# Attention and ternary FFN on eight cores: the first phase shifted by one stage, f and the normalized input transposed by DMA, the ternary weights made in the first phase

## The reference

```python
x = x + attn(layernorm(x))        # x: [8, 4096, 1024] float32
x = x + ffn(layernorm(x))

def attn(x):
    f = x @ W.T + b
    e = f @ f.T + clip(abs(i - j), 0, 10) * 0.01
    return softmax(e, axis=-1) @ f

def ffn(x):
    scale = max(mean(abs(weight)), 1e-5)
    w = clip(round(weight / scale), -1, 1)
    return x @ (w * scale).T
```

## Time and profile before

| what | value |
|---|---|
| median of 3 runs (range) | 1038.83 us (1037.99 to 1039.6) |
| the profiled execution, its own time | 1042.26 us |
| its span, slowest core | 1040.7 us |
| spans of the eight cores | 1024.7 to 1040.7 us |
| TensorE busy | 969.1 us, 93% |
| VectorE busy | 566.4 us, 54% |
| ScalarE busy | 369.7 us, 36% |
| GpSimd busy | 158.9 us, 15% |
| mean granted TensorE clock, slowest core | 0.970 |
| DMA | 186.88 MB, 180 GB/s |

### The profile page before, as it was taken

How to read it: one execution, slowest core, us unless ns; L and a number is a source line. 1 busy time by engine, 2 the same in 40 slices (tenths; PEclk the granted TensorE clock), 3 DMA queues, 4 the chain that set the end, 5 groups by cost and what they waited for, 6 DMA issues and landing times.

```text
span 1040.7 us, 15748 instructions; the slowest of 8 cores (1024.7 to 1040.7 us)
## 1 busy us (share of the span) xinstructions
PE 969.1 (93%) x4958; PEld 471.7 (45%) x4958; DVE 566.4 (54%) x923; ACT 369.7 (36%) x519; POOL 158.9 (15%) x160
## 2 busy tenths in 40 slices
PE   7799999999999979855999999999999999999996
PEld 6354554545445434322444444444444444444442
DVE  5456658685858358453344354545455554556532
ACT  3466656555445645401222323232222222232300
POOL 4000000000000000000001021221324243444530
PEclk9899999999999989978999999999999999999997
DMA  8524423444414656787889897989878888878320
GB/s 230 183 72 135 148 95 139 146 140 149 141 64 157 185 160 212 220 249 215 199 239 234 227 250 211 254 201 249 198 217 227 201 232 180 231 166 236 72 83 40
DMA packets 214897, 186.88 MB, mean 180 GB/s; under 512 B 106656, under 2 KB 181664, under 8 KB 212896
## 3 DMA queue, kind: packets, MB, share of 16 engines
q1 hardware_dynamic: 147584, 127.17, 44.7%
q10 hardware_dynamic: 67200, 58.72, 19.8%
q0 software_dynamic: 32, 0.00, 0.0%
HBM read 109.06 MB, written 51.38 MB: 154 GB/s over the span
## 4 chain that ended last, share of the span: by engine, by line
PE 62%; DVE 12%; SPq 9%; DMA 9%; ACT 4%; issue 3%; DVEq 0%; ACTq 0%
PE pb L652 30%; PE pb L406 12%; PE pb L709 11%; PE pb L359 7%; SPq L281 6%; DMA ln2T<-ln 5%; DVE rm L431 4%; DVE cmax L435 3%; DMA xb<-ft 2%; SPq L345 2%; ACT er L423 1%; PE pt L265 1%; DVE lnb L321 1%; DMA escr<-er 1%; DMA xe<-x 1%
## 5 line engine op out<-in xcount | busy, mean ns | idle before, releaser
L406 PE MATMUL pb<-fT 128*128 128x512 bf16 (+3 forms) x1152 | 242.2, 366 | 0.6 <-ACT fT L369 0.6
L652 PE MATMUL pb<-f,pTa 128*128 128x512 bf16 x1024 | 229.8, 382 | 13.8 <-DVE o L664 13.8
L652 PE MATMUL pb<-f,pTb 128*128 128x512 bf16 x1024 | 229.0, 381 | 0.0
L406 PEld LDWEIGHTS pb<-fT 128*128 128x128 bf16 x1152 | 109.8, 99 | 114.1 <-issue 6.3
L652 PEld LDWEIGHTS pb<-f,pTa 128*128 128x128 bf16 x1024 | 100.8, 100 | 128.4 <-issue 17.1
L652 PEld LDWEIGHTS pb<-f,pTb 128*128 128x128 bf16 x1024 | 100.7, 99 | 114.1 <-issue 2.4
L709 PE MATMUL pb<-wqT,ln2T 128*128 128x512 bf16 x512 | 120.4, 390 | 18.4 <-DVE wqT L777 11.0
L540 ACT ACTIVATE p<-eB,negm 128x3968 bf16<-128x3968 f32 (+30 forms) x31 | 62.1, 2002 | 199.3 <-DMA pTa<-p 99.2
L359 PE MATMUL pb<-ln1T,WT 128*128 128x512 bf16 x512 | 116.8, 388 | 9.3 <-ACT fT L369 7.9
L664 DVE SCALAR_TENSOR_TENSOR o<-pb,st,xres 128x512 f32<-128x512 f32 x64 | 48.0, 751 | 141.9 <-PE pb L652 141.5
L423 ACT COPY er<-pb 128x512 f32<-128x512 f32 (+2 forms) x128 | 69.9, 546 | 79.5 <-PE pb L406 40.9
(11 more groups left out here) (79 smaller groups left out, 631.6 us busy)
## 6 DMA issues: line engine op xcount, KB each, us to landing
escr<-er SPq DMA_DIRECT2D x105, 256.0 KB, 2.3
xres<-x SPq DMA_DIRECT2D x32, 512.0 KB, 5.4
out<-outb SPq DMA_DIRECT2D x32, 512.0 KB, 6.5
xb<-x SPq DMA_DIRECT2D x28, 512.0 KB, 4.3
xb<-ft SPq DMA_DIRECT2D x16, 512.0 KB, 5.6
wst<-wt SPq DMA_DIRECT2D x8, 512.0 KB, 8.8
escr<-eB SPq DMA_DIRECT2D x15, 256.0 KB, 3.2
eB<-escr ACTq DMA_DIRECT2D x2, 1792.0 KB, 11.0
```

Source lines behind the costliest of these rows:

```text
L406: inst = e.matmul(bk[:, 0:n], fT[:, h * S + I * P:h * S + (I + 1) * P], fT[:, h * S + c0:h * S + c0 + n], start=(h == 0), stop=(h == NH - 1))
L652: inst = e.matmul(bank[nb][:, :], pT[I % 2][:, j * P:(j + 1) * P], f_sb[:, j * D + nb * 512:j * D + (nb + 1) * 512], start=(pos == 0), sto ...
```

## The change

- Phase one: chunk 0 and chunk 1 are projected first, in halves of 256 rows (`fproj(c, h, u)`), with the score groups of chunk 0 between them (their evictions, `egroup_out`, emitted later through the list `late`). After that `stage(c)` for c from 1 to 7 emits the score groups of chunk c with the eight `fproj` of chunk c+1 spread evenly between them, and the layer norm of chunk c+2 in single steps at fixed slots.
- `ln1T` has two buffers. Tiles 8 to 31 of the input are transposed by DMA, tiles 0 to 7 still on TensorE. `ftrans(c, h)` is now a DMA transpose of 128 columns by 512 rows, eight per chunk, 64 in all. Row tile 0 of the second layer norm is still transposed on TensorE, in halves (`tail`).
- The stores of score groups with q above 0 are issued by ScalarE instead of SP.
- W is laid out on the host so that each of its eight loads reads whole rows of 4 KB; two of the eight casts go from GpSimd to ScalarE.
- The FFN weight is loaded once, into the buffers of W's float32 copy, in stage 1; `absum` in stage 2, `scale_prep` at its end, `quant` in stages 3 (four), 4 (two) and 5 (two), each slice stored to DRAM, and the whole loaded as bfloat16 (2 MB) into `wqT` after phase one by `wq_load`.
- What waited for the last TensorE instruction of phase one (`e_last_pe`) waits for it and for the DMA transposes of f (`fT_free`).
- Phase two: `ptrans(nn)` is emitted before the FFN of the row tile before and its store, not at the head of the next turn; for row 31 `mfin_col`, `mfin_tmp` and `sub` come at later marks; the tail works in halves of 512 columns with its own banks and stores, and statistics of row 0 come with its halves.

The core of the diff:

```diff
-                [fproj_pe.get(s // 4 - 1)])
+            if s >= 8:
+                xtr_tok[s] = ln1T_tok[s] = tdma(
+                    sl_xt[k], dst, lnb[k][:, :], apply_tok[s],
+                    fproj_pe[s // 4 - 2])
+                return
...
+        def ftrans(c, h):
+            dst = f_sb[:, 4 * c * D:4 * (c + 1) * D].rearrange(
+                "p (s x) -> p s x", s=4)[:, :, h * P:(h + 1) * P]
+            src = fT[:, h * S + c * 512:h * S + (c + 1) * 512]
...
+            t = tdma(sl_ft[c], dst, src, fT_tok[(c, NH - 1, 0)],
+                     fT_tok[(c, NH - 1, 1)], *free)
...
-            ts = SP.dma(slot, lambda e, w: e.dma_start(
+            ts = (ACT if q else SP).dma(slot, lambda e, w: e.dma_start(
...
-                wst[h].rearrange("p (c x) -> p c x", c=NH),
-                wt_d[:, h * P:(h + 1) * P].rearrange("(c p) x -> p c x", p=P)))
+                wst[h][:, :], wt_d[h]))
...
+        def stage(c):
+            es = [(I, q) for I in range(4 * c, 4 * c + 4)
+                  for q in range(nq(I))]
+            if c == NCH - 1:
+                es = [(I, q) for I in (31, 30, 29, 28) for q in range(nq(I))]
+            items = [lambda I=I, q=q: egroup(I, q) for I, q in es]
+            if c + 1 < NCH:
+                step = len(items) / NH
+                for h in range(NH - 1, -1, -1):
+                    items.insert(int(h * step + step / 2),
+                                 lambda h=h: fproj(c + 1, h))
+            n = len(items)
+            if c + 2 < NCH:
+                for k in range(4):
+                    for i, fn in enumerate(tile_tasks(4 * c + 8 + k)):
+                        at_slot(k * n // 4 + i, fn)
+            if c == 1:
+                for k in range(NH):
+                    at_slot(2 * k, lambda k=k: ft_load(k))
+            if c == 2:
+                for k in range(NH):
+                    at_slot(1 + 2 * k, lambda k=k: absum(k))
+                at_slot(n - 1, scale_prep)
+            for c_, i, k in ((3, 1, 0), (3, 4, 1), (3, 13, 2), (3, 19, 3),
+                             (4, 4, 4), (4, 18, 5), (5, 4, 6), (5, 20, 7)):
+                if c == c_:
+                    at_slot(i, lambda k=k: quant(k))
+            if c < NCH - 1:
+                for h in range(NH):
+                    at_slot(n * (h + 2) // 11 + 1, lambda h=h: ftrans(c, h))
...
+        fT_free += [e_last_pe[0]] + [f_tok[4 * c] for c in range(NCH)]
         res_load(31)
         loadE(29)
         rl(31)
         exp_col(30)
         exp_row(30)
         ptrans(30)
+        wq_load()
         loadE(28)
...
-                    ptrans(nx)
                     exp_col(nx)
...
+            if nn >= 0:
+                ptrans(nn)
             if not first:
                 ffn(pv)
-                final(pv)
+                if I:
+                    final(pv)
+        tail()
```

More of the change, by code:

```diff
@@ L422, in egroup, with egroup_out @@
                 free = er_free[r]
+            if late is not None:
+                late.append(lambda: egroup_out(
+                    I, q, i, r, n, c0, dst, slot, free, tp))
+            else:
+                egroup_out(I, q, i, r, n, c0, dst, slot, free, tp)
+        def egroup_out(I, q, i, r, n, c0, dst, slot, free, tp):
+            bk = bank[i]
             ta = ACT.op(lambda e, w: e.copy(dst, bk[:, 0:n]), tp, *free)
@@ L789, in build_nc, with ln_done @@
             x_load(s)
-        for h in range(NH):
+        for h in (1, 3, 4, 5, 6, 7):
             w_cast(h)
+        def ln_done(k, q=None):
+            ln_apply(k)
+            xtrans(k, q)
         ln_stats(0)
+        ln_rs(0)
         ln_stats(1)
-        ln_apply(0)
-        xtrans(0)
-        warm(8)
-        ln_apply(1)
+        ln_rs(1)
+        ln_done(0)
+        warm(9)
         ln_stats(2)
-        xtrans(1)
-        warm(8)
-        ln_apply(2)
+        ln_rs(2)
+        w_cast(0)
@@ L886, in build_nc @@
-        e_last_pe[0] = ftr_pe[NST - 1]
+        ln_rs(3)
+        fproj(0, 0, 0)
+        ln_done(2, DVE)
+        w_cast(2)
+        fproj(0, 1, 0)
+        fproj(0, 2, 0)
+        ln_done(3, DVE)
+        for u, h in ((0, 3), (1, 0), (1, 1), (0, 4), (1, 2), (0, 5), (1, 3),
+                     (0, 6), (1, 4), (1, 5), (0, 7), (1, 6), (1, 7)):
+            fproj(0, h, u)
+        emit_band()
+        late = []
+        ln_stats(4)
+        ln_rs(4)
+        ln_stats(5)
+        ln_rs(5)
+        egroup(0, 0, late)
@@ new lines, in build_nc @@
+        egroup(1, 0, late)
+        ln_done(4)
+        ln_stats(6)
+        ln_rs(6)
+        egroup(2, 0, late)
+        ln_done(5)
+        ln_stats(7)
+        ln_rs(7)
+        egroup(3, 0, late)
+        for fn in late[:2]:
+            fn()
+        fproj(1, 0, 0)
+        ln_done(6)
+        for fn in late[2:]:
+            fn()
+        fproj(1, 1, 0)
+        fproj(1, 2, 0)
+        ln_done(7)
+        for h in range(3, NH):
+            fproj(1, h, 0)
+            if h < 7:
+                fproj(1, h - 3, 1)
+            ftrans(0, h - 3)
@@ L887, in build_nc @@
+        for k in range(4):
+            for fn in tile_tasks(8 + k):
+                fn()
+        for c in range(1, NCH):
+            stage(c)
+        fT_free += [e_last_pe[0]] + [f_tok[4 * c] for c in range(NCH)]
         res_load(31)
@@ L899, in build_nc @@
                 if nx >= 0:
-                    ptrans(nx)
                     exp_col(nx)
                 ln2_moments(pv)
-            if nn >= 0:
+            if nn >= 0 and not first:
                 mfin_col(nn, last_cm)
```

339 lines of the change are left out of this document (178 added, 161 removed).

## The result

The changed kernel takes 1053.29 us (median of four runs, 1052.77 to 1056.91) against 1038.83 before: ratio 1.0147, interval 1.0123 to 1.0171. It is slower by 1.5%, clear of the noise; I had written 972 with 945 to 1002 and gave "slower" 3 in 100. The profiled execution has a span of 1051.6 us on core 3.

The account below looks back on a forecast made before the run. The prediction took TensorE, busy 93% of the span, as the bound. Savings of 32 (phase one), 23 (turn), 5 (later rows) and 6 (tail) took the span from 1040.7 to 975, written as 972 us, range 945 to 1002.

Parts of the forecast that it names:

- less behind it unless VectorE lags: Stages 1 to 7: waits for late tiles about 7 us after stage 1, 2 after stage 2, then less.
- the bounding engine: Phase one: 56 packs moved from TensorE to DMA take 25 us off TensorE, at 0.45 us each.
- Start: Beginning of phase one: stage 1 of the new order starts at 57.
- (a): Start: TensorE's own work before stage 1, 35.5 us from about 16, is done near 52.
- (b): Start: the last tile of chunk 2 is scaled at 50 and landed transposed at 57.
- Stages 1 to 7: Rest of phase one: 36, 37, 45.5, 47.5, 53.5, 59.6 and 53.5 us, 332.6 together.
- Clock: Stage 1: 2 us added for low clock, nothing in the stages behind it.
- The turn: Change to phase two: 75 us with stalls of 9 and clock 2, 23 us less than before.
- Rival 3: The turn does not shrink: p chain and DMA keep rows late, 10 of the 23 us remain, 985; chance 0.12.
- Later rows and tail: Phase two after the turn: 5 us less in the later rows and 6 us less in the tail.
- Rival 4: Stages 1 to 5: new transposes cost SP 5.2 us each like pTa's, 93 us more, 1065, slower; chance 0.03.
- Rival 2: Phase one: SP or DMA sets the pace, stages 1 to 5 lose 7 us more each, 35 in all, 1005; chance 0.15.

Follow-up runs that it names:

- e1: Changed kernel with the layer norm of tiles 8 to 11 emitted in steps between chunk 1's projections: ratio 0.9946 to the kernel before.
- e8: Changed kernel with tiles 8 to 11 interleaved, tiles in earlier slots with later scaling, ternary slices two a stage and ternary rows loaded earlier: ratio 0.9628 to the kernel before.
- e4: Changed kernel with input tiles 8 to 31 transposed on TensorE again (24 packs), f still by DMA: ratio 1.0706 to the kernel before.
- e10: Kernel before, with the 32 transposes of f by DMA instead of packs on TensorE, stage order unchanged: ratio 1.0060.
- e12: e8 with 28 packs of f (stages 0 to 6) back on TensorE: ratio 0.9669, core median 1003 against 1004 of the control.
- e9: Kernel before with two edits of phase two, p's transpose issued ahead of the out store and the tail in halves: ratio 0.9936.
- e11: Kernel before with the attention weights laid out so that each of the eight loads is whole 4 KB rows: ratio 0.9948.
- e6: Changed kernel with tiles 8 to 11 interleaved, tiles in earlier slots, and their root, scaling and transpose one slot later: ratio 0.9774 to the kernel before.
- edit 3: Ternary slices spread two a stage over stages 3 to 6; alone on the changed kernel, core median 1036, 10 us below it.
- the early loads: The eight loads of ternary rows moved before the scores of chunk 0, part of e8; not run apart.
- the later offsets: A tile's root, scaling and transpose one slot later (offsets 0, 2, 3, 4 in place of 0 to 3), part of e6; not run alone.

## Why the prediction was wrong

The step that failed first is how late a tile may be: "less behind it unless VectorE lags", with stalls of 7 and 2 us and then nearly none. Measured were waits of 21.0, 14.3, 6.2, 7.9 and 2.5 us for transposed tiles. The second is that 25 us of packs come off "the bounding engine" in full; the runs show none of them arriving. The third is the clock behind each stall, put at 2 us in all. By part:

**Start, predicted 57, measured 86.6.** Two terms failed. (a) "TensorE's own work up to there is done near 52": it was done at 65.7, with 40.4 us busy instead of 35.5 and 9.4 idle in waits that I had not counted. (b) "The last tile of chunk 2 landed transposed at 57": I reckoned VectorE's time alone. The tile's root needs ScalarE, and in ScalarE's list it stood behind chunk 1's evictions. The diff showed that; I never went through what is queued ahead of L319. The early tile (22 predicted) came at 26.7. Part (b) is worth 11 us of start (e1); the rest of the 30 is (a) and the tiles' own pace, not told apart.

**Stages 1 to 7, predicted 332.6 us together, measured 371.8.** Each stage was the larger of TensorE's and VectorE's load plus a stall. The loads were right (VectorE in stages 3 to 5: 35.9, 39.7 and 45.7 busy with 59, 63 and 73 gaps of 0.1, so 41.8, 46.0 and 53.0 against my 43.6, 47.4 and 53.5). What failed is "less behind it unless VectorE lags": an engine at 0.7 busy lags all the same, when its list asks for a tile's transpose 0 to 4 items before it is needed. In stages 4 and 5 this cost 9.7 and 11.4 us over the forecast. In stage 1, 7.5 over the forecast, it was SP: the last tile was scaled at 117.0 and its transpose issued at 124.1. With lists in better order (e8) the same seven stages take 413.9 - 76.2 = 337.7, 5 from the forecast. So the forecast was right for stages whose tiles have a lead, and this change gives them none.

**Clock, predicted 2 us for stage 1 and nothing behind it.** In the changed kernel one stall near 220 shows this: granted clock of windows of 2 us.

```profile
226.00:228.00 2.00, 2.00 (x6) 0.68 (x5) 0.00 (x0) 0.92 (x2) 0.00 (x0) 0.50 0.00 0
228.00:230.00 2.00, 2.00 (x9) 0.78 (x8) 0.00 (x0) 0.46 (x3) 0.00 (x0) 0.75 0.00 0
230.00:232.00 2.00, 2.00 (x11) 0.94 (x10) 1.24 (x2) 0.91 (x2) 0.00 (x0) 1.00 0.30 116
...
238.00:240.00 2.00, 2.00 (x9) 0.87 (x8) 1.59 (x5) 0.62 (x1) 0.00 (x0) 0.81 1.12 367
```

TensorE works again from 223.3 and gets 1.2 GHz until about 229: 3 us lost; then 2.4 GHz; then 0.81 to 0.86 for 5 us from 236: 1 more. So some 3 to 4 us for every such stall, and phase one had five (ending at 86.6, 130.2, 168.9, 223.3 and 282.0; the one at 168.9 is only 3.9 us long, at the scale's matmul), with a smaller one at 341.4. The whole can be read from e8, which has the same matmuls in phase one (compare the row of the changed kernel in run 4):

```profile
15.00:413.91 398.91, 356.77 (x1848) 177.23 (x1848) 281.58 (x466) 165.41 (x312) 6.81 (x6) 0.97 0.69 187
```

Of the 44.6 us between them 31.7 are idle time (73.9 to 42.1) and 12.8 busy time, which is the clock.

**Packs, "25 us less on the bounding engine".** This step carried the forecast's optimism. TensorE was busy 93% and so I let its time count in full. e10 shows none of 14.4 us arriving in the old order, e12 none of 12.6 in the new; both are packs of f, and for the 24 of the input e4 shows a price, but not in the packs' own time.

**The turn, predicted 75, measured 83.5 (before 98).** The weights' waits did go. TensorE's stalls are 19.2 us where I had 9. "What is late next" was named rightly, the chain of p, but mis-sized: the transpose of p(29) held SP 21.45 us where I had taken's chain plus 5. The same transpose held it 12.12 in the kernel before, in a row that I had not looked at (the earlier trace rows has only the other buffer of pT). I counted 2 MB less of loads, and not that scores, residual, weights and three transposes fall into 40 us of full DMA engines (0.99). Rival 3 (13 of the 23 us lost, 10 kept) had the direction: 8.5 were lost.

**Later rows and tail, predicted 11, measured 11.7.** Right, and e9 makes 7 to 9 of it alone.

**Transposes on SP.** Right: 1.24 to 1.32 us. Rival 4, the only one on the slower side, was priced by a cause that is not there; the Trainium skill's 1309 ns for a block ("VectorE: DVE Perf Modes", "The three transpose paths") is here about what an instruction with four or eight blocks holds SP, and eight blocks land 4.6 to 5.2 us after issue in the median, not eight times 1309 ns. The time came out on its side for another reason. Rival 2 had the size (35 us in stages 1 to 5; measured 32.4 over the forecast there) but laid all of it to SP and DMA. That is the mechanism in stage 1; in stages 4 and 5 SP issues the transpose 1.8 us after the scaling, and there the scaling itself is late.

The sum closes: 975 + 29.6 (start) + 39.2 (stages) + 8.5 (turn) - 0.7 (rest) = 1051.6, the profiled span.

**Where e8's gain over the kernel before lies**, core 5 of both (1029.6 and 1003.8): phase one 422.87 to 414.92, 8.0; from there to the end of the fifth FFN 129.3 to 122.5, 6.8; the rest 477.4 to 466.4, 11.0. The last piece is mostly e9's two edits. Of the first, e11's layout alone can bring 5, so the shift of the stages, the halves and 56 packs fewer are together worth about 3 on this core. Over all eight cores e8 starts phase two 7.7 to 15.1 us earlier, and with the spread of single cores named above those 3 are not told from nothing.

What stays open: whether e8 is faster than e6 at all, and by edit 3 or the early loads (not run apart); what the halves and the later offsets are worth; and what a turn with fewer bytes would give (not tried).

## What to carry to other kernels

Before shifting work between stages, write for each in-order engine what stands ahead of every tiny operation on a cross-engine chain: here two activations of 0.3 us behind thirteen evictions cost 11 us, and a few slots' lead on the tiles was worth 20 us, where the packs of f taken off TensorE were worth nothing. A busy share of 93% does not make an engine the bound; take a part of its load off in one run and see what arrives. A long wait of one engine is not yet the cause: ScalarE's for VectorE stayed while 43 us went; ask what the engine on the path waits for. And the larger of two loads is a floor for a stage: it was the time here only where each chain between the engines had a lead of several items.

## What the runs showed of the hardware

The granted clock of 0.81, with TensorE busy throughout. e10, 128 to 200, core 1, then core 5 (the same kernel in the same execution):

```profile
128.00:200.00 72.00, 72.00 (x312) 31.99 (x310) 42.22 (x72) 29.59 (x54) 0.00 (x0) 0.81 0.49 137
```

```profile
128.00:200.00 72.00, 67.47 (x373) 32.95 (x371) 46.96 (x82) 33.70 (x61) 0.00 (x0) 1.00 0.51 142
```

Cores 0 and 1 stay at 0.81 from 100 to 250, while cores 2 to 7 have 0.94 to 1.00 up to 128 and 0.97 to 1.00 from there. Each window of 4 us from 100 to 120 on core 0 shows 0.81, so this is not a mixture of 0.5 and 1.00 over a stretch, as I had said values between are; core 1 does 312 matmuls where core 5 does 373. The Trainium skill, "TensorE: Matmul & The Clock Gate", section "Seeing it yourself", describes a peak-current limit of 13/16 (0.8125) that takes a whole die while three of its cores are dense. The level agrees with the row; that it takes the whole die does not, as it holds two cores of four here, and in phase two all eight run dense for 500 us at 1.00. It also appears for 5 us, some 7 us after the clock has come back from a stall, as shown above.

And an issue on SP is no fixed price: three transposes of p in the turn hold SP 10 to 21 us, the longest while the DMA engines are full (share 1.04), against 5 in the median of the earlier trace rows.
